# Middle message pass of a four-layer graph network: one-hots and one product of a dot product made by ScalarE in place of VectorE

## What is computed

```python
h = edge_feats                                  # [edges, 8]
for W in (W_mlp1, W_mlp2, W_mlp3):
    h = SILU_2MOM * silu(h @ W / sqrt(W.shape[0]))
w1, w2, w3, w4 = split(h @ W_mlp4 / sqrt(64), 4)  # 4 x 128 path weights of each edge
s0, s1 = x0[sender], x1[sender]                 # [edges, 128] and [edges, 128, 3]
y0, y1 = edge_attrs[:, 0:1], edge_attrs[:, 1:4]
p1 = w1 * s0 * y0
p2 = (w2 * s0)[:, :, None] * y1[:, None, :]
p3 = w3[:, :, None] * s1 * y0[:, None, :]
p4 = w4 * einsum('eum,em->eu', s1, y1) / sqrt(3)
msg = segment_sum(concat(p1, p4, p2, p3), receiver)   # 1024 columns for each node
```

## Time and profile before

| what | value |
| --- | --- |
| median of 3 runs | 2724.3 us |
| the profiled execution: its time | 2719.56 us |
| the profiled execution: span of the program | 2717.9 us |
| busy in the span: PE, DVE, ACT, POOL | 2148.6, 1840.7, 1213.4, 1202.2 us |
| the message pass, from the first tile to the last add | about 1115.5 to 1639.9 us |
| in that stretch, 524.4 us: PE, DVE, ACT, POOL busy | 507.86, 460.48, 217.81, 168.36 us |

### The profile page before, as it was taken

One profiled execution on the slowest core, in us unless ns is written; L12 is line 12 of the kernel. 1 busy time (PEld: TensorE's weight loads), 2 busy tenths in 40 slices (PEclk: granted clock), 3 DMA queues, 4 the chain that ended last, 5 costly groups with the idle time before them and its releaser, 6 DMA issues. The chain is left out here.

```text
span 2717.9 us, 41770 instructions
## 1 busy us (share of the span) xinstructions
PE 2148.6 (79%) x10963; PEld 1101.6 (41%) x10963; DVE 1840.7 (68%) x3929; ACT 1213.4 (45%) x1959; POOL 1202.2 (44%) x1037
## 2 busy tenths in 40 slices
PE   0562555567998995699999995469999999999763
PEld 0331555543443443244444443134555554555321
DVE  8798999922001114588888894359999999999614
ACT  1697000000000111244444441069999999999610
POOL 0570555502730000433333310068888888888400
PEclk9997999978998997799999997789999999999976
DMA  4110100011203221433323321132222222222011
GB/s 193 49 27 5 45 0 0 0 35 43 73 14 99 83 65 42 120 91 94 87 85 94 89 53 39 42 97 78 78 77 72 75 77 69 73 77 77 0 35 46
DMA packets 81449, 169.83 MB, mean 62 GB/s; under 512 B 17306, under 2 KB 43149, under 8 KB 80377
## 3 DMA queue, kind: packets, MB, share of 16 engines
q0 software_dynamic: 35840, 98.88, 13.4%
q1 hardware_dynamic: 45552, 70.25, 7.6%
HBM read 144.93 MB, written 23.98 MB: 62 GB/s over the span
## 5 line engine op out<-in xcount | busy, mean ns | idle before, releaser
L779 PE MATMUL e_two_ps<-w,e_first 128*128 128x512 bf16 x1408 | 420.5, 380 | 0.0
L567 PE MATMUL pairs_ps<-cell_high,src_hot 128*128 128x144 bf16 x1180 | 154.7, 228 | 150.1 <-DVE src_hot L602 108.6
L530 POOL DMA_INDIRECT sorted_records<-edge_record,slot_row x160 | 190.8, 1192 | 174.8 <-POOLq L642 116.5
L779 PE MATMUL e_two_ps<-w,e_first_low 128*128 128x512 bf16 x704 | 267.8, 380 | 0.0
L1534 POOL TENSOR_TENSOR e_first_low<-e_first 128x1024 bf16<-128x1024 f32 x88 | 248.3, 2822 | 19.6 <-DVE e_first L1725 19.5
L1168 POOL COPY u_idx<-src_row 128x4 uint32 (+1 forms) x44 | 8.1, 185 | 556.7 <-DVEq L1332 315.7
L1539 POOL TENSOR_TENSOR e_msg_low<-e_act 128x1024 bf16<-128x1024 f32 x88 | 225.7, 2565 | 56.3 <-DVE e_act L1737 55.5
L1255 ACT ACTIVATE u_msg<-u_t,slot_record 128x128 f32<-128x128 f32 x528 | 172.9, 391 | 126.2 <-DVE u_t L1294 124.8
L1526 POOL DMA_INDIRECT e_got<-src_table,e_idx x176 | 186.1, 1057 | 70.6 <-issue 36.6
L1174 POOL DMA_INDIRECT u_got<-up_table,u_idx x176 | 170.1, 966 | 76.5 <-issue 41.8
L1220 PE MATMUL u_sum_ps<-u_msg,u_hot 128*125 128x512 f32 x352 | 190.3, 622 | 15.1 <-DVE u_msg L1311 15.0
(11 more groups left out here) (316 smaller groups left out, 5004.2 us busy)
## 6 DMA issues: line engine op xcount, KB each, us to landing
rc_w<-in_L_gnn_basis_dram SPq DMA_DIRECT2D x8, 1024.0 KB, 6.6
sorted_records<-pairs SPq DMA_DIRECT2D x5, 1408.0 KB, 17.8
edge_record<-in_edge_floats_dram SPq DMA_DIRECT2D x2, 3125.0 KB
attr_parts<-h SPq DMA_DIRECT2D x22, 256.0 KB, 2.2
e_attrT<-attr_parts SPq DMA_DIRECT2D x44, 128.0 KB
e_dst_all<-dst_row SPq DMA_DIRECT2D x44, 125.0 KB
w<-in_L_gnn_W_dram SPq DMA_DIRECT2D x2, 2048.0 KB
pairs<-in_edge_floats_dram SPq DMA_DIRECT2D x1, 3125.0 KB
```

What stands on the lines that cost most here:

```text
L530: pg.nc.gpsimd.indirect_dma_start(out=pg.sorted, out_offset=bass.IndirectOffsetOnAxis(ap=pg.slot_row[:, j:j + 1], axis=0), in_=pg.edge_rec ...
L567: nc.tensor.matmul(ps[h][:, sb, 0:(COEFS + 1) * CELL], hot, high[:, h, k, :, :].rearrange("p n d -> p (n d)"), start=(k == 0 and sb % 2 == ...
L779: last = nc.tensor.matmul(out, lhsT, rhs, start=(n == 0), stop=(n == len(pairs) - 1))
```

## The change

Two pieces of DVE's work go to ACT.

The one-hots: ACT makes each in two steps from the same row of numbers, |i - d| (Abs, with the negative destination as bias, into a new tile `away`), then Relu(1 - |i - d|), which is 1 where i = d and 0 at every other whole number. It waits for the first step before the second. One one-hot of group g+1 is made behind each tile of group g. DVE still makes the negative destinations, one instruction of 128x4 a group behind tile 2 (`turn_sign`, for group g+2), which waits until ACT has made all one-hots of group g. PE now waits for hot_ready at every tile, not at k = 0 alone.

The first product q = s1[0] y1 of tile k+1: ACT makes it (`inner`) behind tile k's vector_paths and Silu. It waits for the tile's gathered rows and for DVE to be done with the same buffer (four tiles back). DVE's L1298 waits for it (q_first). Semaphore increments (act_passed) stand between ACT's waits and some of its instructions; nobody waits for them.

```diff
@@ in message_pass @@
+        away = pg.sb("u_away", [P, TG, BN], ctx=ctx)
+        minus_dst = pg.sb("u_minus_dst", [P, 2, TG], ctx=ctx)
...
@@ -1214,7 +1217,7 @@
                 t = g * TG + k
                 if k == 0:
                     pe.wait_ge(added, g + 1)
-                    pe.wait_ge(hot_ready, g + 1)
+                pe.wait_ge(hot_ready, t + 1 + 2 * TG)
                 pe.wait_ge(msg_dve, t + 1 + TG)
                 pe.wait_ge(msg_act, t + 1)
                 nc.tensor.matmul(sum_ps[h][0:BN, 0:D], hot[:, h * TG + k, :], msg[:, k, 0:D],
@@ -1251,19 +1254,49 @@
             def vector_paths(g, h, k):
                 t = g * TG + k
                 act.wait_ge(t2_ready, t + 1)
+                act.sem_inc(act_passed, 1)
                 for m in range(3):
                     last = nc.scalar.activation(msg[:, k, (2 + m) * MUL:(3 + m) * MUL], t2[:, k % 2, :], ACT.Copy,
                                                 scale=pg.record[:, bass.ds(t, 1), Y + 1 + m])
                 last.then_inc(msg_act, 1)
+
+            def inner(g, r, k):
+                t = g * TG + k
+                b = r * TG + k
+                act.wait_ge(sems["arrived"][b], sems["before"][b] + (g - r) * (16 // RING) + 16)
+                act.wait_ge(msg_dve, t + 1)
+                act.sem_inc(act_passed, 1)
+                nc.scalar.activation(q[:, k, :], got[:, b, MUL:2 * MUL], ACT.Copy,
+                                     scale=pg.record[:, bass.ds(t, 1), Y + 1]).then_inc(q_first, 1)
+
+            def hot_tile(g, h, k):
+                t = g * TG + k
+                act.wait_ge(scattered, t + 1)
+                if k == 0:
+                    act.wait_ge(minus_made, g + 1)
+                nc.scalar.activation(away[:, k, :], pg.iota_free[:, 0:BN], ACT.Abs,
+                                     bias=minus_dst[:, h, k:k + 1]).then_inc(away_made, 1)
+                act.wait_ge(away_made, t + 1)
+                nc.scalar.activation(hot[:, h * TG + k, :], away[:, k, :], ACT.Relu, scale=-1.0,
+                                     bias=pg.ones[:, 0:1]).then_inc(hot_ready, 1)
 
             def body(g, r, at):
                 for k in range(TG):
                     vector_paths(g, r % 2, k)
                     if k < 3 and at < LAST:
                         layer(g + 1, 1 - r % 2, k)
+                    if k < TG - 1:
+                        inner(g, r, k + 1)
+                    elif at < LAST:
+                        inner(g + 1, (r + 1) % RING, 0)
+                    if at < LAST:
+                        hot_tile(g + 1, 1 - r % 2, k)
 
             for n in range(3):
                 layer(0, 0, n)
+            for k in range(TG):
+                hot_tile(0, 0, k)
+            inner(0, 0, 0)
             four_at_a_time(act, body)
 
         @block.vector
@@ -1273,12 +1306,10 @@
                 nc.vector.tensor_tensor(hid3_low[:, h, :], hid3[:, h, :], upper(hid3[:, h, :]),
                                         ALU.subtract).then_inc(low_made, 1)
 
-            def hot_group(g, h):
-                dve.wait_ge(scattered, g * TG + TG)
-                for k in range(TG):
-                    last = nc.vector.tensor_scalar(hot[:, h * TG + k, :], pg.iota_free[:, 0:BN],
-                                                   pg.dst_in_block[:, bass.ds(g * TG + k, 1)], None, ALU.is_equal)
-                last.then_inc(hot_ready, 1)
+            def turn_sign(g, h):
+                dve.wait_ge(hot_ready, g * TG - TG + 2 * TG)
+                nc.vector.tensor_scalar(minus_dst[:, h, :], pg.dst_in_block[:, bass.ds(g * TG, TG)], -1.0, None,
+                                        ALU.mult).then_inc(minus_made, 1)
 
             def paths(g, r, k, more):
                 t = g * TG + k
@@ -1288,13 +1319,12 @@
                 s0, s1 = got[:, b, 0:MUL], [got[:, b, (1 + m) * MUL:(2 + m) * MUL] for m in range(3)]
                 dve.wait_ge(sems["arrived"][b], sems["before"][b] + (g - r) * (16 // RING) + 16)
                 dve.wait_ge(scattered, t + TG + 1)
-                nc.vector.tensor_scalar(q[:, k, :], s1[0], y[1], None, ALU.mult).then_inc(q_chain, 1)
                 dve.wait_ge(tp_ready, t + 1)
                 dve.wait_ge(msg_act, t)
                 nc.vector.tensor_tensor(t2[:, k % 2, :], tp[:, MUL:2 * MUL], s0, ALU.mult).then_inc(t2_ready, 1)
                 nc.vector.scalar_tensor_tensor(out=msg[:, k, 0:MUL], in0=tp[:, 0:MUL], scalar=y[0], in1=s0,
                                                op0=ALU.mult, op1=ALU.mult)
-                dve.wait_ge(q_chain, 3 * t + 1)
+                dve.wait_ge(q_first, t + 1)
                 nc.vector.scalar_tensor_tensor(out=q[:, k, :], in0=s1[1], scalar=y[2], in1=q[:, k, :],
                                                op0=ALU.mult, op1=ALU.add).then_inc(q_chain, 1)
                 if k == TG - 1 and more:
@@ -1304,10 +1334,10 @@
                     in0=tp[:, 2 * MUL:3 * MUL].rearrange("p (a u) -> p a u", a=1).broadcast_to([P, 3, MUL]),
                     scalar=y[0], in1=got[:, b, MUL:D].rearrange("p (m u) -> p m u", m=3),
                     op0=ALU.mult, op1=ALU.mult)
-                dve.wait_ge(q_chain, 3 * t + 2)
+                dve.wait_ge(q_chain, 2 * t + 1)
                 nc.vector.scalar_tensor_tensor(out=q[:, k, :], in0=s1[2], scalar=y[3], in1=q[:, k, :],
                                                op0=ALU.mult, op1=ALU.add).then_inc(q_chain, 1)
-                dve.wait_ge(q_chain, 3 * t + 3)
+                dve.wait_ge(q_chain, 2 * t + 2)
                 nc.vector.tensor_tensor(msg[:, k, MUL:2 * MUL], tp[:, 3 * MUL:4 * MUL], q[:, k, :],
                                         ALU.mult).then_inc(msg_dve, 1)
                 if k == TG - 1:
@@ -1326,8 +1356,8 @@
                     paths(g, r, k, at < LAST)
                     if k == 1 and at > 0:
                         add(g - 1, 1 - r % 2)
-                    if k == 2 and at < LAST:
-                        hot_group(g + 1, 1 - r % 2)
+                    if k == 2 and at + 1 < LAST:
+                        turn_sign(g + 2, r % 2)
 
             dve.sem_inc(sems["gather_free"], RING * TG)
             dve.sem_inc(msg_dve, TG)
@@ -1336,7 +1366,9 @@
             for to in (w1, w2, w3):
                 nc.vector.memset(to[:, :], 0.0).then_inc(zeroed, 1)
             nc.vector.memset(w4[:, :, :], 0.0).then_inc(zeroed, 1)
-            hot_group(0, 0)
+            dve.sem_inc(hot_ready, 2 * TG)
+            turn_sign(0, 0)
+            turn_sign(1, 1)
             dve.wait_ge(loaded, 16 * 8)
             nc.vector.tensor_copy(w4_parts[:, :, 0, :], w4[:, :, :]).then_inc(parts_made, 1)
             dve.wait_ge(parts_made, 1)
```

More of the change, by code:

```diff
@@ L1129, in message_pass @@
         (zeroed, loaded, parts_made, cleared, hot_ready, scattered, layer_made, layer_done, low_made,
-         tp_ready, t2_ready, q_chain, msg_dve, msg_act, added) = (
+         tp_ready, t2_ready, q_first, q_chain, msg_dve, msg_act, away_made, act_passed, minus_made, added) = (
             ctx.enter_context(nc.semaphore(f"u_{n}")) for n in (
                 "zeroed", "loaded", "parts_made", "cleared", "hot_ready", "scattered", "layer_made",
-                "layer_done", "low_made", "tp_ready", "t2_ready", "q_chain", "msg_dve", "msg_act", "added"))
+                "layer_done", "low_made", "tp_ready", "t2_ready", "q_first", "q_chain",
+                "msg_dve", "msg_act", "away_made", "act_passed", "minus_made", "added"))
         attr_in = [ctx.enter_context(nc.semaphore(f"u_attr_in{h}")) for h in range(2)]
```

## The result

Before 2724.35 us (median of 4 runs, 2723.61 to 2730.34), after 2754.2 us (median of 4, 2751.59 to 2756.95): ratio 1.0105, 95% interval [1.0087, 1.0123]. The change makes the kernel slower by 1.1%. The forecast was 2719.0 with a range up to 2732, so it was wrong.

A forecast was written before the change was run, and what follows sets the result against it. DVE was taken to bound the kernel at 11.91 us a group, and after the change a ring at 11.77. 43 groups gave -6.0 us, the start +0.7, so -5.3 from 2724.3: 2719.0 us, range 2709 to 2732.

The forecast's parts named there:

- What bounds the kernel: Message pass before the change: DVE's gapless stream sets the period of 11.91 us a group.
- PE's floor: Message pass: PE's own work from start to start needs 11.15 us a group, 0.76 us below the period.
- No more than 33 us can come back: Whole pass: relieving DVE can regain at most 0.76 us in each of 43 groups.
- The ring: Message pass: cycle through PE's MLP layer, Silu, `inner`, DVE's messages and PE's scatter becomes the bound, 11.77 us a group.
- Silu 0 to `inner`: ACT, once a group: from Silu 0 to tile 1's first product, 0.33 us, lower bound 0.28, upper 1.17.
- `inner` and on to L1328: ACT to DVE at tile 1: the product itself 0.39 us and hand-over 0.04, together 0.43.
- rival 2: Message pass: PE's third wait and DVE's turn_sign eat the 0.14 us gain; 11.91 us a group, 2724 us; chance 0.15.
- The start: Start of the pass: group 0's one-hots behind the third Silu on ACT delay DVE's first product use by 0.7 us.
- 43 groups x (11.77 - 11.91): Sum over the message pass: the shorter period saves 6.0 us, every group counted alike.
- Rival 1: ACT between Silu 0 and DVE's L1298 of tile 1: `inner` comes later than counted; 2733 to 2755 us; chance 0.15.
- Rival 3: Message pass: `inner` doesn't bind, PE's floor with a 0.1 us stall decides; 11.25 us a group, 2697 us; chance 0.10.
- Rival 4: ACT: Abs or Relu not sharing Silu's table forces table loads at each change of function; +176, 2900 us; chance 0.02.

The follow-up runs named there:

- experiment 6: Kernel after with the first product issued ahead of Silu on ACT, 29 idle DVE increments ahead of the loop; 2757.2 us, ratio 0.9902 to the kernel before.
- experiment 1: Kernel after with 29 idle DVE increments ahead of the loop, putting it where the kernel before has it; 2783.8 us, ratio 0.9998 to the kernel before.
- experiment 2: Kernel before with 170 idle DVE increments ahead of the loop, nothing of the change; 2812.92 us, ratio 1.0109 to the kernel before.
- experiment 8: Kernel after with the first product ahead of Silu on ACT, no idle increments; 2722.09 us against 2723.38, ratio 1.0000 to the kernel before.
- experiment 4: Kernel after with the one-hots back on DVE, product on ACT behind Silu, 16 idle DVE increments; 2747.18 us, ratio 1.0093 to the kernel before.

## Why the prediction was wrong

**What bounds the kernel**: right. DVE set the pace and PE's floor was 11.15 us; experiment 6 reached 11.19. "No more than 33 us can come back": in experiment 6 27 did.

**The ring**: the mechanism was right, one of its terms too small. The parts, from one group of the kernel after (timeline of PE, ACT and DVE):

```profile
1350.60 0.69 PE L1204 MATMUL u_mlp_ps<-u_attrT,u_w 16*128 16x256 f32 x2
...
1357.47 1.12 PE L1223 MATMUL u_sum_ps<-u_msg,u_hot 128*125 128x512 f32 x2 [0.40 <-DVE u_msg L1341]
...
1359.93 1.05 PE L1223 MATMUL u_sum_ps<-u_msg,u_hot 128*125 128x512 f32 x2
...
1362.42 0.69 PE L1204 MATMUL u_mlp_ps<-u_attrT,u_w 16*128 16x256 f32 x2
```

```profile
1351.33 0.38 ACT L1252 ACTIVATE u_hid<-u_mlp_ps 128x256 f32<-128x256 f32 x1 [1.61 <-PE u_mlp_ps L1204]
1351.61 0.39 ACT L1269 ACTIVATE u_q<-u_got,slot_record 128x128 f32<-128x128 f32 x1
```

```profile
1352.14 0.35 DVE L1328 SCALAR_TENSOR_TENSOR u_q<-u_got,slot_record,u_q 128x128 f32<-128x128 f32 x1 [0.89 <-ACT u_q L1269]
...
1355.43 0.28 DVE L1324 TENSOR_TENSOR u_t<-u_tp_ps,u_got 128x128 f32<-128x128 f32 x1
...
1357.05 0.29 DVE L1341 TENSOR_TENSOR u_msg<-u_tp_ps,u_q 128x128 f32<-128x128 f32 x1
```

| term | predicted | here |
| --- | --- | --- |
| MLP layer 0 to Silu 0 | 0.73 | 0.73 |
| Silu 0 to `inner` | 0.33 | 0.28 |
| `inner` and on to L1328 | 0.43 | 0.53 |
| L1328 of tile 1 to tile 2's L1324 | 3.31 | 3.29 |
| to the end of L1341, and to the scatter | 2.04 | 2.04 |
| scatter of tile 2, to that of tile 3 | 2.47 | 2.46 |
| to the next layer 0 | 2.46 | 2.49 |
| sum | 11.77 | 11.82 |

DVE waits 0.89 us at L1328 of tile 1, once a group, and PE 0.40 us at tile 2, as said. The one term off by more than 0.05 is the hand-over from ACT's product to DVE: from the end at 1352.00 to 1352.14, 0.14 us. I had taken 0.04 from the single row where DVE had been waiting at the start of the pass, and that row lies in the straight code. The kernel after has both values: 0.03 in the four groups ahead of the loop and the four behind it, 0.14 in the loop. One of the first groups, ACT's product and DVE's L1328, and then what DVE's sequencer does at L1328 in the group above:

```profile
1138.65 0.39 ACT L1269 ACTIVATE u_q<-u_got,slot_record 128x128 f32<-128x128 f32 x1
```

```profile
1139.07 0.35 DVE L1328 SCALAR_TENSOR_TENSOR u_q<-u_got,slot_record,u_q 128x128 f32<-128x128 f32 x1 [0.61 <-ACT u_q L1269]
```

```profile
L1328 DVEq FUSED_REGOPS  x1: 57/57/57, 1352.0 to 1352.0; - x1
```

In the loop the register operation for L1328 comes only after ACT's product has ended at 1352.00 (it begins at 1352.04), so its 57 ns stand in the hand-over; L1328 has 144 such records for its 176 starts, one for each in the loop and none outside.

Over the rounds of experiment 1 the period is 11.89, and so the 0.14 us a group that were to be gained shrink to 0.02. That is the result of rival 2. PE's third wait and turn_sign don't show in the group above, where the scatter of tile 2 to that of tile 3 takes the predicted time; the 0.07 between its 11.82 and the average of 11.89 is not explained. The comparison itself was uneven as well: 11.91 is an average of groups of 11.82 or 11.83 and one of 12.17 at each round's end, while none of the distances in the ring spans a return.

**The start**: +1.5 us where +0.7 was said. Of the range it is nothing.

**What failed** is a term that the sum put at nothing without a reason: a change in the price of the loop's return. The sum ended with 43 groups x (11.77 - 11.91), as if a group were a group, and the register work and branch at the round's end, seen in the earlier trace rows as part of DVE's 16.8 us ahead of L1291, were carried over at their old price. The edit takes 62 instructions a round out of DVE's loop and 29 from ahead of it, and so moves the loop to another place. There the return takes 2.8 us instead of 0.3, and with the lower clock behind it this costs 3.7 us a return against experiment 1, 29.5 in all. With it the forecast would have been 2748.5, and with the measured ring 2753.7, against 2754.2.

**The rivals.** None of the four had this mechanism. Rival 1 (`inner` comes later) would have given the same time, 2733 to 2755, and that is a trap: by time alone it looks confirmed. The rows speak against it (Silu to `inner` took 0.28 us, less than predicted), and experiment 1 excludes it. Rival 3 was what the better order brings, for its own reason: there the product is out of the ring. Rival 4 is excluded: ACT loads one table for the pass, with Abs and Relu beside Silu. The Trainium skill (ScalarE: Activation LUTs, Table sets: the hidden batching unit) has relu, copy and abs in every set, and the row agrees.

```profile
L1277 ACT ACTIVATE u_away<-iota_free,u_minus_dst 128x125 f32<-128x125 f32 x176 | 68.1, 387 | 0.0
...
L1252 ACT ACT_TABLE_LOAD x1 | 1.3, 1283 | 35.1 <-PEq L1413 35.1
```

**The dearer engine.** Where DVE is the bound, one-hots on ACT gain 0.7%, and both parts in the better order 1.0%: the dearer place costs nothing off the ring. The Trainium skill (ScalarE: Activation LUTs, Rules for kernel authors) would leave relu and multiplication on VectorE. For the single instruction the rows agree (0.20 us on DVE and 0.29 on ACT for a product, in fp32), for the time of this kernel they don't. The loss of time had another cause.

**The signs named** beforehand: DVE's wait of 0.9 us once a group, found, 0.89; DVE's busy time about 60 us lower, found 52.9 (1840.7 to 1787.8); ACT's about 180 higher, found 165.2 (1213.4 to 1378.6); no further table load, found; no wait of PE for the one-hots, found. The period outside 11.65 to 11.95 was named as what would prove me wrong, and 12.71 did.

## What to carry to other kernels

An edit that adds or removes instructions moves the loop in its engine's stream, and a loop of some hundred instructions can stall at every return for that alone; look at the first record behind the branch and at the instruction packets in the queue table before blaming the edited work, and time the edit once more with some idle instructions ahead of the loop. A period averaged over groups hides this: compare the groups of a round one by one. When work goes to another engine, put what the receiver wants soonest ahead of what waits longest: the same product was a loss of 0.9% behind Silu and a gain of 0.5% ahead of it.

## What the runs showed of the hardware that was not expected

- DVE's loop return took 2.8 us instead of 0.3 in three kernels (the kernel after, experiments 2 and 8), with 41 more instruction packets over 8 returns, by place and length of the loop; ACT's and PE's returns in the same rounds did not stall.
- The stall can cost more than it lasts. PE, kept waiting 2.02 us, ran at a granted clock of 0.58 between 1378 and 1382 us. Such a fall cost 1.0 us of the round in experiment 8 and 0.5 in experiment 2. It came behind 8, 6 and 4 of the 8 stalls in the kernel after and experiments 2 and 8, and the length of PE's wait doesn't tell which: in experiment 8 it came after a wait of 2.02 us and not after one of 2.29.
- A product handed from ACT to a waiting DVE took 0.03 us in straight code and 0.14 in the loop (0.14 to 0.15 in experiment 4), where a register operation of 57 ns comes behind the wait.
- An idle semaphore increment on DVE is 21 ns in its record, but 200 of them took 19.1 us, near 0.1 us each.
